# Expert loop of a hybrid block: slot addresses read four at a time by TensorE, three of its waits left out, VectorE's weight copies three steps ahead

## What is computed

```
x = hidden_states.reshape(-1, h)                        # 2048 tokens, 128 channels
shared_out = _swiglu(x, shared_gate_w, shared_up_w, shared_down_w)
logits = x @ gate_w                                     # 32 experts
topk_ids = jnp.argmax(logits, axis=-1)
xs = x * jax.nn.sigmoid(jnp.max(logits, axis=-1))[:, None]
...                                                     # tokens sorted by expert
g = _grouped_mm(sorted_x, routed_gate_w, tokens_per_expert)   # 128 -> 256
u = _grouped_mm(sorted_x, routed_up_w, tokens_per_expert)
d = _grouped_mm(jax.nn.silu(g) * u, routed_down_w, tokens_per_expert)  # 256 -> 128
return (shared_out + d[inv]).reshape(b, s, h)
```

## Time and profile before

| | |
|---|---|
| runs | 605.82, 606.84, 602.8 us; median 605.82 |
| the profiled execution | 604.41 us, its span 602.6 us |
| mean granted TensorE clock | 0.957 of full |
| PE | 527.8 us busy, 88% of the span |
| PEld | 309.6 us, 51% |
| DVE | 430.9 us, 72% |
| ACT | 283.6 us, 47% |
| POOL | 273.9 us, 45% |
| chain that ended last | PE 65%, DVE 23%, issue 6% |
| L1216 in that chain | 8% of the span |

### The profile page before, as it was taken

How to read it: one execution, slowest core, us unless ns; L and a number is a source line. 1 busy time by engine, 2 the same in 40 slices (tenths; PEclk the granted TensorE clock), 3 DMA queues, 4 the chain that set the end, 5 groups by cost and what they waited for, 6 DMA issues and landing times.

```text
span 602.6 us, 17012 instructions
## 1 busy us (share of the span) xinstructions
PE 527.8 (88%) x6418; PEld 309.6 (51%) x6418; DVE 430.9 (72%) x931; ACT 283.6 (47%) x608; POOL 273.9 (45%) x346
## 2 busy tenths in 40 slices
PE   6988978885889989999999999999999766889990
PEld 3323323443543334577767777777766644534330
DVE  3396599988255554888888888998789898245652
ACT  4633443452166651656645554566454242156650
POOL 3467666736426662333344443343322445416661
PEclk9999899998899998999999999999999887799996
DMA  5898900001637844000000000000000000617845
GB/s 169 358 426 159 107 1 2 0 4 34 206 87 218 231 125 123 15 15 20 20 21 21 20 20 21 23 23 21 13 20 8 7 6 31 206 53 221 244 142 156
DMA packets 45329, 54.14 MB, mean 90 GB/s; under 512 B 10880, under 2 KB 36416, under 8 KB 44224
## 3 DMA queue, kind: packets, MB, share of 16 engines
q1 hardware_dynamic: 42688, 47.78, 28.2%
q0 software_dynamic: 2560, 5.26, 2.5%
HBM read 43.55 MB, written 9.48 MB: 88 GB/s over the span
## 4 chain that ended last, share of the span: by engine, by line
PE 65%; DVE 23%; issue 6%; ACT 2%; DMA 2%; POOL 1%; SPq 0%; DVEq 0%; POOLq 0%; ACTq 0%
PE psum L1216 8%; PE psum L1639 7%; PE psum L1621 7%; PE psum L1712 5%; PE psum L1232 4%; PE psum L1691 4%; PE psum L1223 3%; PE psum L1133 3%; PE psum L1142 3%; PE psum L1660 3%; DVE arena L757 2%; PE psum L1592 2%; PE psum L274 2%; DVE arena L751 2%; PE psum L275 2%
## 5 line engine op out<-in xcount | busy, mean ns | idle before, releaser
L2100 POOL TENSOR_TENSOR arena<-arena 128x512 f32<-128x512 f32 x32 | 40.4, 1285 | 112.5 <-issue 103.9
L1412 POOL DMA_INDIRECT y_tok<-arena,to x48 | 56.3, 1173 | 60.5 <-ACT arena L1280 55.8
L1806 ACT ACTIVATE arena<-psum 128x512 f32<-128x512 f32 x64 | 38.1, 597 | 47.3 <-PE psum L1621 44.3
L1621 PE MATMUL psum<-arena 128*128 128x512 f32 x128 | 59.2, 605 | 0.7 <-ACT arena L1789 0.7
L1216 PE MATMUL psum<-experts,arena 128*32 x96 | 50.0, 603 | 1.9 <-issue 0.9
L1216 PE MATMUL psum<-arena 128*32 128x512 f32 x288 | 50.9, 605 | 0.0
L657 POOL TENSOR_TENSOR arena<-arena 128x512 f32<-128x512 f32 x32 | 37.2, 1181 | 27.8 <-DVE arena L757 17.5
L1347 DVE COPY arena<-psum 128x256 f32<-128x256 f32 x48 | 20.4, 424 | 40.7 <-PE psum L1223 39.7
L1639 PE MATMUL psum<-arena 128*128 128x128 f32 x384 | 47.5, 278 | 0.8 <-ACT arena L1811 0.8
L1285 ACT ACTIVATE arena<-experts 128x768 f32 x48 | 40.4, 845 | 13.2 <-issue 13.0
L1639 PEld LDWEIGHTS psum<-arena 128*128 128x128 f32 x384 | 45.2, 192 | 1.8 <-ACT arena L1811 1.8
(11 more groups left out here) (237 smaller groups left out, 1212.0 us busy)
## 6 DMA issues: line engine op xcount, KB each, us to landing
arena<-in_experts SPq DMA_DIRECT2D x48, 384.0 KB
experts<-in_experts SPq DMA_DIRECT2D x8, 1536.0 KB, 17.3
arena<-sorted_x SPq DMA_DIRECT2D x48, 64.5 KB
sorted_x<-zeros SPq DMA_DIRECT2D x2, 1536.0 KB, 14.6
arena<-in_w_qkv SPq DMA_DIRECT2D x16, 192.0 KB, 2.7
arena<-y_tok SPq DMA_DIRECT2D x8, 256.0 KB, 3.6
x_tok<-in_x SPq DMA_DIRECT2D x4, 256.0 KB, 3.9
arena<-in_w_out SPq DMA_DIRECT2D x16, 64.0 KB, 1.9
```

The lines of the kernel that those rows point to most:

```text
L1412: pool.indirect_dma_start(out=y_tok, out_offset=bass.IndirectOffsetOnAxis(ap=f_to[:, s:s + 1], axis=0), in_=f_gy[s % 4], in_offset=None).t ...
L1621: pe.matmul(ring("in", n, j)[:, :], b_w[n % 2][:, which * P:which * P + P], x, start=True, stop=True)\
L1806: act.activation((b_q, b_k)[which][:, part * CHUNK:part * CHUNK + CHUNK], src, ACT.Copy, scale=(D_B ** -0.5, 1.0)[which]).then_inc(h["drai ...
L2100: pool.tensor_tensor(b_yn[:, part], b_y[:, part], b_rec[:, part], ALU.mult).then_inc(h["normed"], 1)
```

## The change

Four things are changed, all in the expert loop:

- `find` is called in every fourth step and reads four addresses with one load. For that the addresses are stored by j: slot j of step s stands at j x 24 + s. VectorE's cast writes them so, and the other engines read at the new places.
- On TensorE `find` moves behind `turn_in`, directly ahead of `gate_up`.
- TensorE's `gate_up` waits for w_act only in steps 0 and 1 and for w_dve in steps 0 to 2; `down` waits for y_copied only in the last two steps. The other waits of TensorE cover these by the order in which ScalarE and VectorE work.
- VectorE copies the weights of three steps before its loop, and in step s those of s + 3.

```diff
--- before.py
+++ after.py
@@ -47,6 +47,7 @@
 SLOTS = 96
 SIDE = P // SLOT_ROWS
 RUNS = SLOTS * SLOT_ROWS // P
+FOUND = 4
 ROW = C + 1
 ROUNDER = 1.5 * 2.0 ** 28
 HALF_TILES = TILES // 2
@@ -1196,7 +1197,9 @@
             expert_at = {}
 
             def find(s):
-                expert_at[s] = pe.value_load(f_slot_at[0:1, SIDE * s:SIDE * s + 1], min_val=0, max_val=(EXPERTS - 1) * WROW)
+                _, values = nc.values_load_multi_w_load_instructions(
+                    f_slot_at[0:1, s:s + FOUND], [pe.engine], min_val=0, max_val=(EXPERTS - 1) * WROW)
+                expert_at.update(zip(range(s, s + FOUND), values))
 
             def side_weights(s, at, n):
                 return (experts[:, bass.ds(expert_at[s] + at, n)], f_w_act[s % 5][:, at:at + n],
@@ -1208,8 +1211,10 @@
 
             def gate_up(s):
                 done(pe, "gxt", s + 1)
-                done(pe, "w_act", s + 1)
-                done(pe, "w_dve", s + 1)
+                if s < 2:
+                    done(pe, "w_act", s + 1)
+                if s < 3:
+                    done(pe, "w_dve", s + 1)
                 pe.wait_ge(w_slot[s % 6], 16 * (RUNS // 6 * k + s // 6 + 1))
                 for j, weights in enumerate(side_weights(s, 0, 2 * INNER)):
                     rows = slice(SLOT_ROWS * j, SLOT_ROWS * j + SLOT_ROWS)
@@ -1225,7 +1230,8 @@
 
             def down(s):
                 done(pe, "sht", s + 1)
-                done(pe, "y_copied", s - 1)
+                if s >= RUNS - 2:
+                    done(pe, "y_copied", s - 1)
                 for half in range(2):
                     for j, weights in enumerate(side_weights(s, 2 * INNER + half * C, C)):
                         rows = slice(half * P + SLOT_ROWS * j, half * P + SLOT_ROWS * j + SLOT_ROWS)
@@ -1234,10 +1240,10 @@
                 mm.then_inc(t["y"], 1)
 
             for s in range(-1, RUNS + 2):
-                if 0 <= s < RUNS:
-                    find(s)
                 if s + 1 < RUNS:
                     turn_in(s + 1)
+                if 0 <= s < RUNS and s % FOUND == 0:
+                    find(s)
                 if 0 <= s < RUNS:
                     gate_up(s)
                 if 0 <= s - 2:
@@ -1281,7 +1287,7 @@
 
             def copy_weights(s):
                 done(act, "y", s - 4)
-                at = act.value_load(f_slot_at[0:1, SIDE * s + 1:SIDE * s + 2], min_val=0, max_val=(EXPERTS - 1) * WROW)
+                at = act.value_load(f_slot_at[0:1, 1 * RUNS + s:1 * RUNS + s + 1], min_val=0, max_val=(EXPERTS - 1) * WROW)
                 act.activation(f_w_act[s % 5], experts[:, bass.ds(at, WROW)], ACT.Copy).then_inc(t["w_act"], 1)
 
             done(act, "rows", 1)
@@ -1329,7 +1335,7 @@
             product_shared(dve, k, late)
             done(dve, "slot_row", 1)
             chain(dve.tensor_scalar(f_slot_row[0:1, :], bank[7][0:1, 0:SLOTS], float(WROW), None, ALU.mult))
-            dve.tensor_copy(f_slot_at[0:1, :], f_slot_row[0:1, :]).then_inc(t["rows"], 1)
+            dve.tensor_copy(f_slot_at[0:1, :].rearrange("o (j s) -> o s j", j=SIDE), f_slot_row[0:1, :].rearrange("o (s j) -> o s j", j=SIDE)).then_inc(t["rows"], 1)
             for c in range(late, STEPS):
                 add_shared(dve, k, c)
                 if c + 1 < STEPS:
@@ -1348,20 +1354,20 @@
 
             def copy_weights(s):
                 done(dve, "y", s - 4)
-                at = dve.value_load(f_slot_at[0:1, SIDE * s + 2:SIDE * s + 3], min_val=0, max_val=(EXPERTS - 1) * WROW)
+                at = dve.value_load(f_slot_at[0:1, 2 * RUNS + s:2 * RUNS + s + 1], min_val=0, max_val=(EXPERTS - 1) * WROW)
                 dve.tensor_copy(f_w_dve[s % 5], experts[:, bass.ds(at, WROW)]).then_inc(t["w_dve"], 1)
 
             done(dve, "rows", 1)
             dve.wait_ge(loaded_experts, 16 * EXPERT_LOADS)
-            for s in range(2):
+            for s in range(3):
                 copy_weights(s)
             for s in range(0, RUNS + 1):
                 if s >= 1:
                     copy_h(s - 1)
                 if s < RUNS:
                     product(s)
-                if s + 2 < RUNS:
-                    copy_weights(s + 2)
+                if s + 3 < RUNS:
+                    copy_weights(s + 3)
             done(dve, "down", STEPS)
 
         def add_experts(dve, k, c):
@@ -1421,7 +1427,7 @@
 
             def weights(s):
                 done(sp, "y", s - 5)
-                at = sp.value_load(f_slot_at[0:1, SIDE * s + 3:SIDE * s + 4], min_val=0, max_val=(EXPERTS - 1) * WROW)
+                at = sp.value_load(f_slot_at[0:1, 3 * RUNS + s:3 * RUNS + s + 1], min_val=0, max_val=(EXPERTS - 1) * WROW)
                 sp.dma_start(f_w[s % 6], w["experts"][:, bass.ds(at, WROW)]).then_inc(w_slot[s % 6], 16)
 
             def fetch(s):

```

## The result

The changed kernel takes 607.28 us (median of 17 runs, 600.66 to 610.46), the kernel before, measured beside it, 604.02 us (17 runs, 601.52 to 607.2). The ratio is 1.0045, with a 95% interval of 1.0024 to 1.0065: within 1% of no change, and 3 us on the slower side. The ratio leaves out two of the changed kernel's 17 executions, which were in a slower state. The profiled execution took 608.05 us, with a span of 606.3, against 604.41 and 602.6 before.

The account below looks back on a forecast made before the run. A ring of waits through GpSimd's scatter, which delays word of TensorE's results, was taken to bound the loops. Finds +0.7, starts +0.2, other steps -0.3 sum to +0.6 on 605.82: 606.4 us, range 598.5 to 613.0.

Parts of the forecast that it names:

- the start: First steps of each loop: the find of four ahead of the first gate_up, +0.2 us for both loops, from -0.3 to +1.6.
- The find's size: On TensorE's sequencer: a find of four takes about 1.4 us, each further value 0.27 us, directly before gate_up.
- The cover: In the loops' steps with a find, the scatter hides most of the delay; 0.7 us shows, between 0 and 5.
- the 5 us that were priced bare: Ten steps with a find of four inside the loops, 0.5 us each if nothing hides the delay.
- If steps with a find grow to 3 us, B or C does: Sign to look for in the loops' step times: such growth would mean Rival B or Rival C holds.
- late telling: In the loops, TensorE results finished inside a scatter reach the copying engines late, 1.1 and 0.8 us after they are ready.
- VectorE, the columns and the left-out waits: In the expert loop: copies, new address places and dropped waits, 0; up to 0.3 us credited for steps without a find.
- The array's gap: Between TensorE's products: gaps at tiling changes belong to the array; were they the sequencer's, 2 to 3 us more won.
- Rival A: In the loops: TensorE's own address load makes the lateness, the scatter only stands beside it; 599 us, chance 0.24.
- Rival B: In the loops: a scatter has two telling moments and finds push results past the first; +7.4 us, 613.2, chance 0.15.
- Rival C: Before gate_up: register work is the find's price, heaped up without cover; 5 us remain, 611 us, chance 0.06.
- The other thought under C: On TensorE: row ends are estimates, so the product may be late in the array, not the telling; time as Rival C.

Follow-up runs that it names:

- changed_again: The changed kernel without an edit, run again in the second place: 594.61 us beside 587.41 for the kernel before, ratio 1.0109.
- warm_start: The changed kernel with one extra matmul ahead of the first find of four of each loop: 594.85 us beside 587.41, ratio 1.0114.
- single_finds: The changed kernel with one find of one address in each step, ahead of turn_in, the rest of the change kept: 586.43 us, ratio 0.9962.
- before_no_find: The kernel before with TensorE's address read replaced by a fixed expert number, so a quarter of the rows take other weights: 585.13 us, ratio 0.9961.
- before_again: The kernel before without an edit, run again in the second place: 587.47 us, ratio 1.0011.
- first_find_early: The changed kernel with each loop's first find of four moved ahead of the waits for the shared feed-forward and experts: 591.59 us beside 588.26, ratio 1.0058.
- only_find_of_four: The changed kernel with the left-out waits and VectorE's third copy ahead taken back: 596.10 us beside 588.26, ratio 1.0133.
- after_plain_store: The changed kernel with GpSimd's scatter replaced by plain stores from SyncE, so routed rows land at other tokens: 595.35 us, ratio 1.0127.
- find_of_two: The changed kernel with two addresses read by one load in every second step: 593.45 us, ratio 1.0118.

## Why the prediction came out as it did

The time (606.4 predicted, 607.28 measured) and the sign of nothing over 1% were right, the time partly by luck. The forecast was +0.6 us on a median of three runs, 605.82; the 17 runs beside the changed kernel have 604.02. So the change is +3.3 us by the medians and +2.7 by the ratio (1.0024 to 1.0065), where +0.6 (1.001) was forecast, and a base 1.8 us too high hides over half of the difference. The missing 2 to 3 us stand in one term, the start. The steps one by one:

**The find's size held.** "About 1.4 us" is 1.46 to 1.72 from the load's start to the last check in the changed kernel's two traces; the interval from `down` to `gate_up` in a step with a find, "about 1.9 us", is 1.67 to 2.19 with a mean of 1.94. The 0.27 us for each further value is 0.28 between register instructions.

**The cover held, in the first place.** "The work that hides it is the scatter" is what the trace there shows, if it is read over more than one step. A find delays one `down`; its result is told with the scatter all the same, and the next step is short. By the prediction's own numbers a step with a find takes 1.9 + 0.89 = 2.8 us and the next one 2.37 - 0.43 = 1.94; measured are 3.02 and 1.91. The results behind the ten finds end 0.44 to 1.35 us behind a scatter's start and are told 1.38 to 1.46 behind it, as results that end early in a scatter are. What is left of the 5 us that were priced bare, and of the 7.5 that ten finds cost where nothing is told late, is 0.5 us from `gate_up` to `gate_up` or 1.0 from scatter to scatter, against 0.7 - 0.3 = 0.4 forecast. The two loops differ by 1.1 us in this (the first gains 0.3 or 0.1 us, the second loses 0.8 or 1.1), so the 0.1 us of agreement are no measurement. "If steps with a find grow to 3 us, B or C does" was a bad sign: the forecast itself has them at 2.8. That late telling is what covers rests on the traces of both places and on ratios whose intervals do not meet (1.0045 and 1.0109); the places may differ in more, and no run with late telling was to be had for a test.

**The start was mis-sized by the clock.** The term was +0.2 us for both loops, bound +1.6; measured 3.4. Without the clock it is near its size (+0.2 for each loop instead of +0.1, in changed_again's second loop and in warm_start). What it left out is that a longer idle time ahead of `gate_up` can be followed by a fall of the granted clock, which cost 1.5 to 1.6 us each time that it came. This term is nearly the whole difference between the two profiled executions.

**VectorE, the columns and the left-out waits** were put at 0 apart from the third copy; single_finds shows a gain of 2 us (0.9962) for all of them. The third copy ahead brings 0.25 to 0.35 at each start, as the bound said; the rest I can't place in a trace.

**The array's gap** was right. Here the Trainium skill, "TensorEngine Tiling (Array Packing)", "Key Properties", had it that a change of the tiling mode drains the engine; before_no_find agrees so far: with nothing on the sequencer the interval of 1.03 us from `down` to `gate_up` does not shrink, so its gaps are not the sequencer's.

**Rival A** (the lateness is made by TensorE's own load) is refuted twice. In the changed kernel 36 of 48 steps have no load and many are told 1.1 us late. In before_again all 48 have one and none is told over 0.37 us late. My forecast's own sentence, that what ends within a scatter is told late, fits, but its two copies "0.09 and 0.14 us after its end" do not make the scatter's end the moment: at 176.09 the scatter ended after 0.98 us, at 177.07, and the copy started at 177.54. The telling mostly comes 1.3 to 1.5 us behind the scatter's start, however long its row is. **Rival B**'s two moments exist: in the changed kernel results that end 0.22 us into a scatter are told at 0.58 to 0.84 us behind its start or at 1.32 to 1.36, and those behind a find all at the later one. Its bill of 7.4 us did not come: the `down` after such a result follows 1.92 us behind the one before in eight of ten cases, 2.06 and 2.18 in the others. **Rival C** (the heap without cover, +5 us) is what the second place shows: +7.2 us, 1.4 times its price, 1.6 us of it by the clock in the profiled execution. There the same change would have been forecast wrongly by my argument. The other thought under C, that the product is late in the array and not in the telling, is refuted by the semaphores' times: L1216, behind the late-told rows, ends and is told on time.

## What to carry to other kernels

Reading several values by one load saves the loads and none of the register work, and puts that work in one place: price it as a heap against the work that the array still has when the heap begins (here 1.03 us in front of `gate_up`, 1.7 behind it), and put it where that is longest; where nothing was told late, ten such heaps cost 5 to 7 us in front of `gate_up` (first_find_early against single_finds, and the steps of changed_again) and some 1 us behind it. A longer step is not yet a loss: where a ring of waits sets the pace, measure from one turn of the ring to the next. A stall that one trace shows may belong to the place it was taken in, so a saving or a cover that rests on it should be given as two cases. When something is added in front of a stage's first matmul, look at the granted clock behind it as well.

## What was not expected of the hardware

- The same program takes 604 us in one place and 587 in another at nearly the same mean clock (0.957 and 0.964 in the profiled runs), and 12.1 of the 17.9 us lie in the two loops with scatters. TensorE's results that end beside a scatter are mostly told 1.3 to 1.5 us behind its start in one, in the step of the earlier trace rows three of them within 0.08 us, while TensorE itself runs on schedule; in the other they are told at once (semaphore within 0.07 us of the row's end in before_again), from the same phase. Why, stays open, and so does whether it is the chip: the second place is two chips that agree.
- A load of two addresses took 532 to 728 ns, one of four 327 to 577, one of one 295 to 497.
- Idle times of TensorE of 1.47 to 1.70 us in front of a loop were followed by 3.4 us at half clock in four of eight starts (the changed kernel in both places, only_find_of_four, after_plain_store). In the starts with shorter ones (up to 1.35 us, find_of_two) it did not fall.
